# Index columns read in place, with a waited-for write of zeros between indirect transfers

## The chip, the cores and the metric

One core of a Trainium2 chip runs the whole program. The metric is the device time of one execution in microseconds (us). The kernel before takes 4911.03 us (median of three runs, 4899.02 to 4911.47). Everything below is read from one profiled execution of 4916.42 us.

## The reference

The input is a graph of 100,000 nodes with 64 features and 50,000 directed edges `src[e] -> dst[e]`, sorted by `dst`. Four blocks follow each other, each of the form "normalise, message passing, add":

```
h = relu(layernorm(x));  x = x + hop(hop(h))              # hop: segment_sum(edge_weight * h[src], dst)
h = relu(layernorm(x));  x = x + gcn(h @ W)               # degree-normalised sum, with self loops
h = relu(layernorm(x));  x = x + mlp(h + segment_sum(h[src], dst))
h = relu(layernorm(x));  x = x + update([h, segment_sum(message([h[src], h[dst], edge_attr]), dst)])
```

Rows of `x` have to be fetched by node number, and rows of the result have to be stored by node number. Both are done with indirect transfers, of which the program issues more than 2,700.

## The kernel before

The edges are laid out as 128 partitions by T = 392 columns; a unit is G = 14 columns, a step is two units (b = 0 and 1), and there are 14 steps per pass over the edges. An indirect transfer handles one column: 128 rows of 64 floats, one row for each partition, at the row numbers that stand in one column of an index tile. So a unit needs 14 gathers, and a pass 392.

GpSimd (POOL) issues every indirect transfer, in an order written out by hand. It passes through these stretches:

- From 25 us on, four units of rows of `x` are gathered (`gather_by_column`, call at L949), then `hop0` (L951 to L969) alternates accumulating scatters with gathers whose index slots VectorE has filled. `hop1` (L991 to L1005) holds accumulating scatters alone, up to about 2,116 us.
- 2,122 to 2,780 us: the first pass over the edges with gathered rows (loop at L1010, k = 0, table `xu`, index `map_idx`).
- 2,836 to 3,541 us: the same loop with k = 1, table `table0`, index `ptr_i`.
- 3,581 us to the end: the last pass. `t_gather` (L1046) gathers a step's rows from `table1` by `ptr_i`, `t_scatter` (L1053) stores a step's finished rows into `out` by `out_idx`. They take turns: gather of step i + 2 after scatter of step i - 1.

In the last three stretches, and at the very start, the 14 transfers of a unit are issued in the same way: `slot_copy` (L923 to L925) copies one index column (128 x 1 integers) from the wide tile (`dstc_i`, `map_idx`, `ptr_i` or `out_idx`) into a slot (`isl` or `osl`), raises `s_slot`, POOL waits for it, and issues the transfer with the slot as its index (L929 for gathers, L1062 for scatters). There are 1,624 such pairs of copy and transfer: 56 at the start, 392 in each of the two passes, and 784 in the last one.

What POOL waits for ahead of a unit: in the k = 0 pass, that VectorE has used the rows of the step before (`centred`); in the k = 1 and the last pass, `ga_free`, raised by VectorE when it has read the gathered rows. `t_scatter` waits for `o_ready` (the rows in `acc` are finished) and, from the second step on, also for `written[b]`: the scatters of the step before with the same slot have landed (L1058). ScalarE, which fills `acc`, waits for the same `written[b]` before it fills (L1666).

While POOL does this, VectorE, ScalarE and TensorE compute the rows of the nodes and edges step by step. VectorE's long operations are on 128 x 896 floats (a unit). Some take both inputs from SBUF (L2204, L2231, L2237), others one from SBUF and one from PSUM (L2214, L2222), others a single input (reductions, L2187).

Of the kernel before, what the change touches and what calls it, by code (L numbers as in the profile page):

```python
# [5 lines left out]
P = 128  # L6
# [8 lines left out]
G = 14  # L15
U = T // G
STEPS = U // 2
# [140 lines left out]
def gnn(nc, x, src, dst, edge_attr, edge_weight, W1g, b1g, W2a, b2a, W2b, b2b, mW1, mb1, mW2, mb2, uW1, ub1,  # L158
        uW2, ub2, out):
    ctx = ExitStack()  # L160
    with ctx:
        def sb(name, shape, dt=F32):
            return ctx.enter_context(nc.sbuf_tensor(name, shape, dt))

        def sem(name):
            return ctx.enter_context(nc.semaphore(name))

        def dram(name, shape):
            return nc.dram_tensor(name, shape, F32, kind="Internal").ap()


        tables = [dram(f"table{k}", [ROWS + P, D]) for k in range(2)]
# [48 lines left out]
        out_idx = sb("out_idx", [P, T], I32)  # L221
        dstc_i = sb("dstc_i", [P, T], I32)
        ptr_i = sb("ptr_i", [P, T], I32)
# [15 lines left out]
        hin, xw, h, vt, ga = (pair(n, unit) for n in ("hin", "xw", "h", "vt", "ga"))  # L239
# [4 lines left out]
        acc = pair("acc", unit)  # L244
# [25 lines left out]
        isl, osl = (pair(n, [P, G], I32) for n in ("isl", "osl"))  # L270
        isl_of = [*isl, *pair("isl_ahead", [P, G], I32)]
        hsum = sb("hsum", [P, D])
        fix = sb("fix", [P, 2 * D])
        brd = sb("brd", [P, 3 * D])
        bz = sb("bz", [P, 2 * P])
# [14 lines left out]
        ga_of = [*(t[:, :, :] for t in ga), ccu[0][2], ccu[1][2]]  # L290
# [87 lines left out]

        s_asked = sem("prep_operands_ready")
        s_answer = sem("prep_products_in_psum")  # L380
        s_slot = sem("pool_slot_copied")
        s_turned = sem("keys_turned")
        s_krow = sem("key_rows_ready")
        s_kept = [sem(f"edge_nodes_stored{b}") for b in range(2)]
# [68 lines left out]
        class Dense:  # L453
# [15 lines left out]
            copied = Ticks(sem("dense_copied"), [("h2", 0), ("y3", 1), ("h3", 1), ("h3", 0), ("y3", 0), ("h1", 1), ("h1", 0), ("h2", 1)],  # L469
                            [("h2", 0), ("y3", 1), ("h3", 1), ("h3", 0), ("y3", 0)])  # L470
# [13 lines left out]
        for k in range(2):  # L484
            sums = per_unit("m") if k == 0 else [("m", b, q) for b in B2K for q in range(HB)]
            f = Phase(f"hop{k}", [("l", B2K)] if k == 0 else [], per_unit("m"),
                      picked=per_half if k == 0 else None, compared=per_half,
                      merged=sums, sums=sums, slot=per_unit("i") if k == 1 else None,
                      in_free=per_unit("x") if k == 1 else None)
# [10 lines left out]
        for k in range(2):  # L500
            v = per_unit("v") if k == 1 else None
            v_back = v[::-1] if k == 1 else None
            f = Phase(f"s{k}", [("l", B2K)], v_back, turned=v_back, copied=v_back, product=v, taken=v,
                      ga_free=per_unit("g")[::-1] if k == 1 else None,
                      state_ready=per_unit("x"), acc_ready=per_unit("a"))
# [11 lines left out]
        tt = Phase("t", [("d1", B2K), ("d2", B2K), ("s3", B2K), ("d3", B2K)],  # L517
                   [*per_unit("vd", "us"), ("agg", 0), *per_unit("ud"), ("agg", 1), *per_unit("h3")],
                   turned=T_TURNED, copied=T_TURNED,
                   product=per_unit("m0", "m1", "vd", "us", "ud", "u0", "u1"),  # L520
                   hidden=T_MLP, second=T_MLP, message=per_unit("m0", "m1"),
                   taken=per_unit("vd", "us", "ud", "u0", "u1"), acc_ready=per_unit("a"),
                   in_free=per_unit("x"), gx_free=per_unit("g"), ga_free=per_unit("g"), o_ready=per_unit("o"),
                   early=T_EARLY, n=STEPS)
# [43 lines left out]
        def ecol(i, b):  # L568
            return (2 * i + b) * G

        def tcol(i, b):
            return (U - 1 - b) * G - 2 * G * i
# [287 lines left out]
        def _(pool):  # L860
            after = Settled(pool, s_passed)
# [58 lines left out]

                    after.wait_ge(s_sorted, 4 * 16 * SG * i + 4 * 16 * SG)

            def slot_copy(o, i_):  # L923

                return nc.gpsimd.tensor_copy(o, i_).then_inc(s_slot, 1)  # L925

            def gather(o, table, idx, s, columns=range(G)):
                for g in columns:
                    nc.gpsimd.indirect_dma_start(  # L929
                        o[:, g, :], None, table, bass.IndirectOffsetOnAxis(idx[:, g:g + 1], 0)).then_inc(s, 16)  # L930


            def gather_by_column(o, table, slot, index, c, s, copied):

                for g in range(G):
                    slot_copy(slot[:, g:g + 1], index[:, c + g:c + g + 1])
                    after.wait_ge(s_slot, copied + g + 1)
                    gather(o, table, slot, s, (g,))
                return copied + G

            after.wait_ge(s_node, 1)
            copied = 0

            hop_max, all_max = pool.to_reg(ROWS + 4 * P - 1), pool.to_reg(ROWS + N + 4 * P - 1)
            f = hops[0]
            for u in range(4):
                copied = gather_by_column(ga_of[u], x, isl_of[u], dstc_i, u * G, f.got[u], copied)  # L949

            def hop0(i):  # L951
                for b in B2K:
# [60 lines left out]
            for k, f in enumerate(sp_):  # L1013
                if k == 0:
                    table, index = xu, u_i
                else:
                    table, index = tables[k - 1], ptr_i
                    for b in B2K:
                        after.wait_ge(sp_[0].kept[b], 2 * 16 * STEPS)

                def body(i, first, copied):
                    for b in B2K if k == 0 else B2K[::-1]:
                        if not first:

                            if k == 0:
                                after.wait_ge(*f.centred.at(i - 1, ("l", b)))
                            else:
                                after.wait_ge(*f.ga_free.at(i - 1, ("g", b)))
                        copied = gather_by_column(ga[b], table, isl[b], index, ecol(i, b), f.got[b], copied)
                    return copied  # L1030

                for i in range(STEPS):
                    copied = body(i, i == 0, copied)

                for b in B2K:
                    after.wait_ge(f.stored[b], 16 * STEPS)
                nc.gpsimd.indirect_dma_start(hsum[:, :], None, tables[k], bass.IndirectOffsetOnAxis(head_i[:, :], 0),
                                             bounds_check=rows_max, oob_is_err=False).then_inc(s_head, 16)
                after.wait_ge(s_fix, k + 1)
                nc.gpsimd.indirect_dma_start(tables[k], bass.IndirectOffsetOnAxis(head_i[:, :], 0), fix[:, 0:D], None,  # L1040
                                             bounds_check=rows_max, oob_is_err=False).then_inc(s_fixed, 16)
                pool.dma_start(rows(tables[k])[:, EC * D:T * D], fix[:, D:2 * D]).then_inc(s_fixed, 16)
                after.wait_ge(s_fixed, 32 * (k + 1))


            def t_gather(i, copied, first=False):  # L1046
                for b in B2K:
                    if not first:
                        after.wait_ge(*tt.ga_free.at(i - 1, ("g", b)))
                    copied = gather_by_column(ga[b], tables[1], isl[b], ptr_i, tcol(i, b), tt.got_a[b], copied)  # L1050
                return copied

            def t_scatter(i, copied, first=False):  # L1053
                for b in B2K:
                    after.wait_ge(*tt.o_ready.at(i, ("o", b)))
                    if not first:

                        after.wait_ge(tt.written[b], 16 * G * i)  # L1058
                    for g in range(G):
                        slot_copy(osl[b][:, g:g + 1], out_idx[:, tcol(i, b) + g:tcol(i, b) + g + 1])  # L1060
                        after.wait_ge(s_slot, copied + b * G + g + 1)
                        nc.gpsimd.indirect_dma_start(  # L1062
                            out, bass.IndirectOffsetOnAxis(osl[b][:, g:g + 1], 0), acc[b][:, g, :], None,
                            bounds_check=nodes_max, oob_is_err=False).then_inc(tt.written[b], 16)
                return copied + 2 * G

            for q in LANES:
                after.wait_ge(s_dense[q], 16 * DSTEPS)
            copied = t_gather(0, copied, True)
            copied = t_gather(1, copied)  # L1070
            copied = t_gather(2, copied)
            copied = t_scatter(0, copied, True)
            copied = t_gather(3, copied)
            for i in range(2, STEPS - 2):
                copied = t_scatter(i - 1, copied)
                copied = t_gather(i + 2, copied)
            for i in (STEPS - 3, STEPS - 2):
                copied = t_scatter(i, copied)

            for b in B2K:  # L1080
                after.wait_ge(tt.kept[b], 16 * STEPS)
            nc.gpsimd.indirect_dma_start(hsum[:, :], None, suffix, bass.IndirectOffsetOnAxis(tail_i[:, :], 0),
                                         bounds_check=rows_max, oob_is_err=False).then_inc(s_head, 16)
            t_scatter(STEPS - 1, copied)
            after.wait_ge(s_border, 5)
            nc.gpsimd.indirect_dma_start(out, bass.IndirectOffsetOnAxis(brd_i[:, :], 0), fix[:, 0:D], None,
                                         bounds_check=nodes_max, oob_is_err=False).then_inc(s_final, 16)
# [1626 lines left out]
```

## Time and profile before

| | |
|---|---|
| median of three runs | 4911.03 us |
| profiled execution, its own time | 4916.42 us |
| its span, first to last instruction | 4914.2 us |
| POOL busy | 3807.9 us (77%) |
| PE (TensorE) busy | 3612.6 us (74%) |
| DVE (VectorE) busy | 3039.2 us (62%) |
| ACT (ScalarE) busy | 2012.8 us (41%) |
| granted TensorE clock, mean | 0.766 of full speed |

The profile names for each idle time of an engine what ended it, and follows the chain of work that ended last from the end of the program to its beginning. A duration of POOL in the profile is the time an instruction is recorded with; for an indirect transfer it is the time in which POOL makes the transfer's descriptors, not the time in which the data move. "issue" is time in which an engine waited for nothing that the profile shows.

### The profile page before, as it was taken

To read this page: it belongs to the slowest core of one execution; us is meant where nothing else is said; L and a number is where in the kernel's file an instruction comes from. 1 tells how busy PE (TensorE), PEld (TensorE's weight loads), DVE (VectorE), ACT (ScalarE), POOL (GpSimd) and SP (SyncE) were. 2 spreads that over 40 slices of the span, in tenths; PEclk is the share of its full clock that TensorE was granted. 3 is DMA by queue.
4 is the path that set the end of the run, shared out by engine and by line. 5 is a ranking of instruction groups with operands and counts; after the bars stand their busy time and mean duration, and the time that the engine had idled before them with its cause. 6 is when DMAs were issued, how large, how long until landed. Compare 5 with 4: busy or idle time off the path is not lost.

```text
span 4914.2 us, 62117 instructions
## 1 busy us (share of the span) xinstructions
PE 3612.6 (74%) x18706; PEld 2888.8 (59%) x18706; DVE 3039.2 (62%) x7232; ACT 2012.8 (41%) x5132; POOL 3807.9 (77%) x4405
## 2 busy tenths in 40 slices
PE   4767666666499999957777778878458787778784
PEld 2444344444399989945555556666346665656663
DVE  5634444444456566658888858888557666566661
ACT  3434434434311111135555555656225454454452
POOL 6788888888778888877788558888677888888875
PEclk8667767766655555578898989999779898998896
DMA  8433333332344454433343324444333223232220
GB/s 285 100 56 45 56 56 45 57 56 28 50 91 86 83 92 84 55 71 123 104 133 104 117 78 156 153 149 164 131 99 111 67 84 100 71 112 68 71 69 20
DMA packets 335499, 452.19 MB, mean 92 GB/s; under 512 B 208111, under 2 KB 233301, under 8 KB 334740
## 3 DMA queue, kind: packets, MB, share of 16 engines
q1 hardware_dynamic: 159268, 361.69, 20.9%
q0 software_dynamic: 176000, 87.72, 15.5%
q8 instruction: 109, 1.79, 0.2%
q14 instruction: 122, 1.00, 0.1%
HBM read 258.41 MB, written 225.53 MB: 98 GB/s over the span
## 4 chain that ended last, share of the span: by engine, by line
POOL 38%; issue 14%; PE 10%; DVE 6%; DMA 2%; ACT 2%; DVEq 0%; SPq 0%; POOLq 0%; ACTq 0%; another core or an unknown queue 0%
POOL ga L929 19%; POOL out_x L1062 8%; POOL isl L925 5%; POOL xu L1002 3%; PE tp L1259 2%; PE tp L1246 2%; POOL osl L925 2%; PE mm L1104 2%; PE mm L1123 1%; DMA xu<-acc,osl 1%; DVE xf L1948 1%; DVE wide L2107 1%; PE mm L1135 1%; PE mm L1097 1%; ACT zx L1597 1%
## 5 line engine op out<-in xcount | busy, mean ns | idle before, releaser
L929 POOL DMA_INDIRECT ga<-table,isl x784 | 838.8, 1070 | 224.4 <-issue 113.7
L1002 POOL DMA_INDIRECT xu<-acc,osl x392 | 625.1, 1595 | 144.8 <-issue 106.2
L1209 PE MATMUL tp<-xw,cc 128*128 128x394 f32 x784 | 411.5, 623 | 334.7 <-DVE cc L2015 243.3
L929 POOL DMA_INDIRECT ga<-xu,isl x392 | 424.1, 1082 | 111.8 <-POOL isl L925 61.5
L1062 POOL DMA_INDIRECT out_x<-acc,osl x392 | 418.6, 1068 | 114.5 <-POOL osl L925 80.8
L1209 PEld LDWEIGHTS tp<-xw,cc 128*128 128x128 f32 x784 | 141.3, 220 | 592.6 <-issue 324.9
L1246 PE MATMUL tp<-us,wide 128*128 128x64 f32 x1568 | 416.9, 422 | 88.9 <-DVE us L2143 50.0
L1246 PEld LDWEIGHTS tp<-us,wide 128*128 128x128 f32 x1568 | 379.9, 332 | 93.7 <-DVE us L2143 50.2
L1259 PE MATMUL tp<-acc,wide 128*128 128x64 f32 x1560 | 423.1, 427 | 0.8
L1194 PE MATMUL tp<-us,wide 128*128 128x64 f32 x1568 | 343.9, 421 | 69.6 <-DVE us L1932 60.8
L1562 ACT ACTIVATE acc<-tp,h 128x64 f32<-128x64 f32 x392 | 101.7, 310 | 693.2 <-PE tp L1259 541.9
L965 POOL DMA_INDIRECT hop_even<-acc,osl x196 | 322.1, 1643 | 81.2 <-issue 56.4
L1259 PEld LDWEIGHTS tp<-acc,wide 128*128 128x128 f32 x1560 | 371.8, 328 | 20.6 <-ACT acc L1562 5.8
L1194 PEld LDWEIGHTS tp<-us,wide 128*128 128x128 f32 x1568 | 337.8, 332 | 76.5 <-issue 76.5
L965 POOL DMA_INDIRECT hop_odd<-acc,osl x196 | 318.2, 1623 | 60.9 <-issue 57.9
L1097 PE MATMUL mm<-ident,wide 128*128 128x128 f32 x1176 | 196.8, 321 | 127.3 <-DVE wide L2204 59.0
L1104 PE MATMUL mm<-cc,u1s 128*128 128x512 f32 x448 | 213.7, 603 | 97.5 <-ACT zx L1597 76.1
L2055 DVE TENSOR_TENSOR osl<-sm,spare 128x14 int32<-128x14 f32 x28 | 4.9, 174 | 435.0 <-DMA hop_odd<-acc,osl 223.2
L1527 ACT ACTIVATE hin<-tp,xw 128x391 bf16<-128x391 f32 x392 | 233.0, 594 | 98.1 <-PE tp L1209 97.1
L1097 PEld LDWEIGHTS mm<-ident,wide 128*128 128x128 f32 x1176 | 167.0, 171 | 165.6 <-issue 88.8
L1540 ACT COPY acc<-tp 128x896 f32<-128x896 f32 x28 | 25.3, 905 | 580.7 <-DMA hop_odd<-acc,osl 256.6
L925 POOL COPY isl<-ptr_i 128x1 int32<-128x1 int32 x784 | 221.6, 283 | 50.8 <-DVE us L2231 40.0
(377 smaller groups left out, 9733.1 us busy)
## 6 DMA issues: line engine op xcount, KB each, us to landing
wide<-xu SPq DMA_DIRECT2D x84, 448.0 KB
zx<-key_rows SPq DMA_DIRECT2D x28, 896.0 KB
out_x<-wide SPq DMA_DIRECT2D x56, 448.0 KB
table<-acc SPq DMA_DIRECT2D x56, 448.0 KB
xf<-xs SPq DMA_DIRECT2D x56, 448.0 KB
wide<-table SPq DMA_DIRECT2D x56, 448.0 KB
xu<-in_x SPq DMA_DIRECT2D x25, 1000.0 KB
hop_even<-zeros SPq DMA_DIRECT2D x1, 12544.0 KB
```

Source lines behind the costliest of these rows:

```text
L925: return nc.gpsimd.tensor_copy(o, i_).then_inc(s_slot, 1)
L929: nc.gpsimd.indirect_dma_start(o[:, g, :], None, table, bass.IndirectOffsetOnAxis(idx[:, g:g + 1], 0)).then_inc(s, 16)
L965: nc.gpsimd.indirect_dma_start(hop[odd], bass.IndirectOffsetOnAxis(osl[b][:, g:g + 1], 0), acc[b][:, g, :], None, compute_op=ALU.add).then ...
L1002: nc.gpsimd.indirect_dma_start(xu, bass.IndirectOffsetOnAxis(osl[b][:, g:g + 1], 0), acc[b][:, g, :], None, compute_op=ALU.add).then_inc(f ...
L1062: nc.gpsimd.indirect_dma_start(out, bass.IndirectOffsetOnAxis(osl[b][:, g:g + 1], 0), acc[b][:, g, :], None, bounds_check=nodes_max, oob_i ...
L1097: t = nc.tensor.transpose(o[0:w, j * P:j * P + P], blk, ident[:, :])
L1104: t = nc.tensor.matmul(o[:, c:c + n], weights, flat(src_)[:, c:c + n], start=True, stop=extra is None)
L1194: t = nc.tensor.matmul(o[:, g * D:g * D + D], equal[b][:, c, (g % 2) * P:(g % 2) * P + P], us[b][:, c, :], start=n == 0, stop=n == 1)
L1209: f.key_row.raise_by(nc.tensor.matmul(tp[1][:, at:at + KEYS], reach[:, g * P:g * P + P], key_steps, start=True, stop=True), ("g", b, g))
L1246: t = nc.tensor.matmul(o, equal_run[:, 2 * q + n, mine:mine + P], us[b][:, 2 * q + n, :], start=n == 0, stop=alone and n == 1)
L1259: t = nc.tensor.matmul(o, equal_run[:, c, 2 * P + mine:3 * P + mine], passed[:, c, :], start=False, stop=n == 1)
L1527: nc.scalar.activation(sign_out[:, 2 * (g % 2), 0:EC], tp[1][:, at + 3:at + KEYS], ACT.Sign, bias=key_high[:, column], scale=-1.0, accum_o ...
```

## The change

The column copy goes. A transfer's index is now the column of the wide tile itself. In the copy's place, and in the same place of POOL's order, stands a write of zeros over a 128 x 128 float tile, `spacer`, which nothing reads. It raises the semaphore that the copy raised (renamed), and the transfer waits for it as before. In `t_scatter` the wait for `written[b]` goes as well, since no slot is overwritten. The slots `isl` and `osl` stay for `hop0` and `hop1`.

```
-            def slot_copy(o, i_):
-
-                return nc.gpsimd.tensor_copy(o, i_).then_inc(s_slot, 1)
...
-            def gather_by_column(o, table, slot, index, c, s, copied):
+            def gather_spaced(o, table, index, c, s, spaced):
 
                 for g in range(G):
-                    slot_copy(slot[:, g:g + 1], index[:, c + g:c + g + 1])
-                    after.wait_ge(s_slot, copied + g + 1)
-                    gather(o, table, slot, s, (g,))
-                return copied + G
+                    nc.gpsimd.memset(spacer[:, :], 0.0).then_inc(s_slot, 1)
+                    after.wait_ge(s_slot, spaced + g + 1)
+                    gather(o, table, index[:, c:c + G], s, (g,))
+                return spaced + G
...
-            def t_scatter(i, copied, first=False):
+            def t_scatter(i, spaced):
                 for b in B2K:
                     after.wait_ge(*tt.o_ready.at(i, ("o", b)))
-                    if not first:
-
-                        after.wait_ge(tt.written[b], 16 * G * i)
                     for g in range(G):
-                        slot_copy(osl[b][:, g:g + 1], out_idx[:, tcol(i, b) + g:tcol(i, b) + g + 1])
-                        after.wait_ge(s_slot, copied + b * G + g + 1)
+                        nc.gpsimd.memset(spacer[:, :], 0.0).then_inc(s_slot, 1)
+                        after.wait_ge(s_slot, spaced + b * G + g + 1)
                         nc.gpsimd.indirect_dma_start(
-                            out, bass.IndirectOffsetOnAxis(osl[b][:, g:g + 1], 0), acc[b][:, g, :], None,
+                            out, bass.IndirectOffsetOnAxis(out_idx[:, tcol(i, b) + g:tcol(i, b) + g + 1], 0),
+                            acc[b][:, g, :], None,
                             bounds_check=nodes_max, oob_is_err=False).then_inc(tt.written[b], 16)
```

POOL's row in the last pass, where the gathers of a unit end and the scatters of a step begin, before (`isl1` and `osl0` are the slots of unit 1 and unit 0):

```order
L929 DMA ga1<-table1,isl1 128x64 [waits pool_slot_copied]
L925 COPY isl1<-ptr_i 128x1
L929 DMA ga1<-table1,isl1 128x64 [waits pool_slot_copied]
L925 COPY osl0<-out_idx 128x1 [waits t_rows_written0,t_o_ready]
L1062 DMA out_x<-acc0,osl0 100000x64 [waits pool_slot_copied]
L925 COPY osl0<-out_idx 128x1
```

and the same place after the change:

```order
L926 DMA ga1<-table1,ptr_i 128x64 [waits pool_spacer_written]
L933 MEMSET spacer 128x128
L926 DMA ga1<-table1,ptr_i 128x64 [waits pool_spacer_written]
L1054 MEMSET spacer 128x128 [waits t_o_ready]
L1056 DMA out_x<-acc0,out_idx 100000x64 [waits pool_spacer_written]
L1054 MEMSET spacer 128x128
```

Each copy has become a write in its place; no transfer has moved, and the one wait for `t_rows_written` ahead of a step's scatters is gone. POOL has 3,718 rows in both orders, and the other engines keep theirs.

## Rows read from the trace of the kernel before

**Rows 1.** The page's chain that ended last, shares of the span by line.

```profile
POOL ga L929 19%; POOL out_x L1062 8%; POOL isl L925 5%; POOL xu L1002 3%; PE tp L1259 2%; PE tp L1246 2%; POOL osl L925 2%; PE mm L1104 2%; PE mm L1123 1%; DMA xu<-acc,osl 1%; DVE xf L1948 1%; DVE wide L2107 1%; PE mm L1135 1%; PE mm L1097 1%; ACT zx L1597 1%
```

**Rows 2.** Chain that ended last in 2122:2780, 2836:3541, 3740:4730, 4730:4914, shares of each.

```profile
by line: POOL ga L929 32.3%; issue 15.8%; POOL isl L925 7.9%; PE mm L1104 5.9%; PE mm L1123 3.7%; PE mm L1097 3.1%; ACT zx L1597 2.7%; PE mm L1135 2.6%; DMA ga<-xu,isl 2.3%; DVE st L2248 2.0%; ACT wide L1608 2.0%; DVE wide L2218 2.0%; DVE a
by line: POOL ga L929 56.1%; POOL isl L925 16.8%; issue 16.0%; PE mm L1123 2.1%; PE mm L1104 1.7%; PE mm L1097 1.3%; DMA hin<-ms 1.1%; PE mm L1135 0.9%; ACT wide L1608 0.5%; ACT zx L1597 0.4%; ACT cc L1589 0.4%; DMA ga<-table,isl 0.3%; DVE 
by line: POOL out_x L1062 33.3%; POOL ga L929 32.7%; issue 17.9%; POOL osl L925 8.3%; POOL isl L925 7.9%; POOLq L117 0.0%
by line: POOL out_x L1062 45.5%; issue 13.9%; POOL osl L925 10.0%; PE mm L1104 7.9%; PE mm L1123 4.9%; DMA out_x<-acc,osl 2.3%; ACT acc L1669 1.9%; DVE zx L1948 1.9%; PE tp L1097 1.7%; DVE st L2412 1.1%; ACT vt L1500 0.9%; POOLq L161 0.7%; 
```

**Rows 3.** Column copies (L925) by stretch: us, POOL busy (count), PEclk, DMA share, GB/s.

```profile
2122.00:2780.00 658.00, 105.08 (x392) 0.89 0.36 112
2836.00:3541.00 705.00, 122.75 (x392) 0.88 0.44 143
3740.00:4730.00 990.00, 156.07 (x614) 0.90 0.28 85
4730.00:4914.00 184.00, 17.83 (x83) 0.75 0.09 23
```

**Rows 4.** Copies by form in 2122:2780, 2836:3541, 3581:4914 (twice): busy us, mean ns.

```profile
L925 POOL COPY isl<-map_idx 128x1 int32<-128x1 int32 x392 | 105.4, 269 | 18.1 <-DVE xc L2255 13.6 <-DMA xu<-hsum 1.2
L925 POOL COPY isl<-ptr_i 128x1 int32<-128x1 int32 x392 | 122.8, 313 | 43.8 <-DVE us L2231 40.0 <-DMA table<-fix 1.3
L925 POOL COPY osl<-out_idx 128x1 int32<-128x1 int32 x392 | 99.2, 253 | 59.3 <-DVEq L80 57.5
L925 POOL COPY isl<-ptr_i 128x1 int32<-128x1 int32 x392 | 98.8, 252 | 7.0 <-DVEq L80 3.2 <-DMA table<-fix 1.3
```

**Rows 5.** All copies of L925: duration ns minimum/median/maximum, first and last start.

```profile
L925 POOL COPY isl<-ptr_i x784: 183/194/1111, 2835.9 to 4727.7; 128x1 int32<-128x1 int32 x196
L925 POOL COPY isl<-map_idx x392: 181/191/1116, 2121.7 to 2777.8; 128x1 int32<-128x1 int32 x196
L925 POOL COPY osl<-out_idx x392: 178/192/1164, 3734.0 to 4903.0; 128x1 int32<-128x1 int32 x196
```

**Rows 6.** Timeline of POOL and DVE near 3004 to 3014 us: start, us taken.

```profile
3003.63 1.09 DVE L2204 SCALAR_TENSOR_TENSOR wide<-wide,st 128x896 f32<-128x896 f32 x1
3003.74 1.02 POOL L925 COPY isl<-ptr_i 128x1 int32<-128x1 int32 x1
...
3005.03 0.97 POOL L929 DMA_INDIRECT ga<-table,isl  x1 [0.27 <-POOL isl L925]
...
3010.60 1.08 DVE L2231 TENSOR_TENSOR us<-hin,ga 128x896 f32<-128x896 f32 x1
...
3010.80 1.73 POOL L929 DMA_INDIRECT ga<-table,isl  x1 [0.27 <-issue]
...
3013.00 0.97 POOL L929 DMA_INDIRECT ga<-table,isl  x1 [0.27 <-POOL isl L925]
...
3013.43 1.09 DVE L2204 SCALAR_TENSOR_TENSOR wide<-wide,st 128x896 f32<-128x896 f32 x1
```

**Rows 7.** POOL's writes of constants at the start: start, us taken.

```profile
2.67 0.10 POOL L864 MEMSET kn_i<- 128x1 int32 x1
2.70 0.42 POOL L865 MEMSET wt<- 128x392 f32 x1
...
3.47 0.20 POOL L867 MEMSET ones<- 128x128 f32 x1
```

**Rows 8.** Two gathers with bounds whose index is a column of a tile.

```profile
L1082 POOL DMA_INDIRECT hsum<-suffix,tail_i x1 | 1.0, 1035 | 1.5 <-DMA suffix<-cc 1.5
L985 POOL DMA_INDIRECT fix<-hop_odd,ptr_i x1 | 1.0, 1022 | 0.3 <-issue 0.3
```

**Rows 9.** Waits in total, times, longest: for gathered rows, and for landed scatters.

```profile
DVE us L2231 <- DMA ga<-table,isl: 39.6, 12, 8.6
ACT acc L1669 <- DMA out_x<-acc,osl: 83.3, 8, 17.5
```

More of the change, by code:

```diff
@@ L272, in gnn @@
         hsum = sb("hsum", [P, D])
+        spacer = sb("spacer", [P, P])
         fix = sb("fix", [P, 2 * D])
@@ L380, in gnn @@
         s_answer = sem("prep_products_in_psum")
-        s_slot = sem("pool_slot_copied")
+        s_slot = sem("pool_spacer_written")
         s_turned = sem("keys_turned")
@@ L930, in gather @@
                         o[:, g, :], None, table, bass.IndirectOffsetOnAxis(idx[:, g:g + 1], 0)).then_inc(s, 16)
-            def gather_by_column(o, table, slot, index, c, s, copied):
+            def gather_spaced(o, table, index, c, s, spaced):
                 for g in range(G):
-                    slot_copy(slot[:, g:g + 1], index[:, c + g:c + g + 1])
-                    after.wait_ge(s_slot, copied + g + 1)
-                    gather(o, table, slot, s, (g,))
-                return copied + G
+                    nc.gpsimd.memset(spacer[:, :], 0.0).then_inc(s_slot, 1)
+                    after.wait_ge(s_slot, spaced + g + 1)
+                    gather(o, table, index[:, c:c + G], s, (g,))
+                return spaced + G
             after.wait_ge(s_node, 1)
-            copied = 0
+            spaced = 0
             hop_max, all_max = pool.to_reg(ROWS + 4 * P - 1), pool.to_reg(ROWS + N + 4 * P - 1)
@@ L948, in _ @@
             for u in range(4):
-                copied = gather_by_column(ga_of[u], x, isl_of[u], dstc_i, u * G, f.got[u], copied)
+                spaced = gather_spaced(ga_of[u], x, dstc_i, u * G, f.got[u], spaced)
             def hop0(i):
@@ L1019, in _, with body @@
                         after.wait_ge(sp_[0].kept[b], 2 * 16 * STEPS)
-                def body(i, first, copied):
+                def body(i, first, spaced):
                     for b in B2K if k == 0 else B2K[::-1]:
@@ L1028, in body @@
                                 after.wait_ge(*f.ga_free.at(i - 1, ("g", b)))
-                        copied = gather_by_column(ga[b], table, isl[b], index, ecol(i, b), f.got[b], copied)
-                    return copied
+                        spaced = gather_spaced(ga[b], table, index, ecol(i, b), f.got[b], spaced)
+                    return spaced
                 for i in range(STEPS):
-                    copied = body(i, i == 0, copied)
+                    spaced = body(i, i == 0, spaced)
                 for b in B2K:
@@ L1043, in _, with t_gather @@
                 after.wait_ge(s_fixed, 32 * (k + 1))
-            def t_gather(i, copied, first=False):
+            def t_gather(i, spaced, first=False):
                 for b in B2K:
@@ L1049, in t_gather @@
                         after.wait_ge(*tt.ga_free.at(i - 1, ("g", b)))
-                    copied = gather_by_column(ga[b], tables[1], isl[b], ptr_i, tcol(i, b), tt.got_a[b], copied)
-                return copied
-            def t_scatter(i, copied, first=False):
+                    spaced = gather_spaced(ga[b], tables[1], ptr_i, tcol(i, b), tt.got_a[b], spaced)
+                return spaced
+            def t_scatter(i, spaced):
                 for b in B2K:
                     after.wait_ge(*tt.o_ready.at(i, ("o", b)))
-                    if not first:
-                        after.wait_ge(tt.written[b], 16 * G * i)
@@ L1064, in t_scatter @@
                             bounds_check=nodes_max, oob_is_err=False).then_inc(tt.written[b], 16)
-                return copied + 2 * G
+                return spaced + 2 * G
             for q in LANES:
                 after.wait_ge(s_dense[q], 16 * DSTEPS)
[L1069 to L1073, printed above, removed]
+            spaced = t_gather(0, spaced, True)
@@ L1074, in _ @@
+            spaced = t_gather(1, spaced)
+            spaced = t_gather(2, spaced)
+            spaced = t_scatter(0, spaced)
+            spaced = t_gather(3, spaced)
             for i in range(2, STEPS - 2):
-                copied = t_scatter(i - 1, copied)
-                copied = t_gather(i + 2, copied)
+                spaced = t_scatter(i - 1, spaced)
+                spaced = t_gather(i + 2, spaced)
             for i in (STEPS - 3, STEPS - 2):
-                copied = t_scatter(i, copied)
+                spaced = t_scatter(i, spaced)
@@ L1083, in _ @@
                                          bounds_check=rows_max, oob_is_err=False).then_inc(s_head, 16)
-            t_scatter(STEPS - 1, copied)
+            t_scatter(STEPS - 1, spaced)
             after.wait_ge(s_border, 5)
```

## The prediction

> **What bounds the kernel now.** I read the chain of work that ended last first. It is the only view that says whose time is the program's time: POOL's gathers, scatters and column copies are the largest named entries on it, the copies alone at 5% and 2% of the span [rows 1]. The change touches only POOL in three passes, so the same chain is read by stretch next. In the k = 0 pass (2122 to 2780 us) it runs through POOL for about half the time, and through PE, ACT and DVE for the rest; in the k = 1 pass and between 3740 and 4730 us it is practically POOL alone [rows 2]. To see how many of the copies lie on it, take the chain's share of each stretch against all copies there [rows 2, 3]:
>
> - k = 0: 7.9% of 658 us is 52 us, of 105.08 us busy: 49% of 392 copies, about 194.
> - k = 1: 16.8% of 705 us is 118 us, of 122.75 us: 96%, about 378.
> - 3740 to 4730: 8.3% and 7.9% of 990 us are 160 us, against 156.07 us: all 614.
> - 4730 to the end: 10.0% of 184 us is 18 us, against 17.83 us: all 83.
>
> That makes 1,269 pairs on the path. The 56 pairs at the start and those from 3581 to 3740 us I count as off it.
>
> The third view is the copies' durations. The median is 191 to 194 ns and the longest over 1.1 us [rows 5], yet the means are 269, 313, 253 and 252 ns [rows 4]. A copy of one column has no reason to take a microsecond, so something holds it. The timeline of POOL beside DVE shows what: a copy that starts 0.11 us after a 1.09 us operation of DVE with two inputs in SBUF (L2204) takes 1.02 us and ends with it. The gather that starts at 3010.80, inside L2231 (both inputs in SBUF, until 11.68), takes 1.73 us instead of 0.97. But the gather of 3013.00 is in the middle of its work when L2204 begins at 3013.43, and still takes 0.97 us [rows 6]. So what waits is POOL's read, of the column or, at the start of a transfer, of the index; what POOL writes afterwards (the descriptors) passes.
>
> **The change, part by part.**
>
> *Removed: the copy's read.* The excess of the copies over their median is 392 x (269 - 191) ns = 30.6 us, 392 x (313 - 194) ns = 46.6 us, and for the last pass 392 x (253 - 192) and 392 x (252 - 194) ns, together 46.6 us [rows 4, 5]. On the path are 49%, 96% and 697/784 of that: 15 + 45 + 41 = 101 us. The new instruction reads nothing, so I take it that it is not held. Not all of the 101 us is won, because DVE's operation may still be running when the transfer reads its index. From the copy's place to that read go 0.20 us of the write, 0.27 us to the transfer's start, and about 0.12 us (the gather of 3010.80 was lengthened by 0.76 us, while DVE's operation had 0.88 us to run) [rows 6, 7]: 0.59 us. An operation of 1.09 us, met at a random point, has on average 0.545 us left, and beyond 0.59 us it has on average 0.50 x 0.50 / (2 x 1.09) = 0.115 us: 21% moves on to the transfer. I take a quarter, since transfers that used to start just after a held copy now meet DVE's operations at random. Gain: 0.75 x 101 = 76 us.
>
> *Added: the write of zeros.* A 128 x 128 write took 0.20 us (0.204 in the list of groups), against the copy's 0.192: 12 ns more, 1,269 x 0.012 = 15 us. The trace shows none behind a transfer. From the other side: a one-column write is recorded with 0.10 us, but the next one starts 0.03 us after it [rows 7], so up to 0.07 us of a recorded duration can lie beside a neighbour. If it did here, a pair would be 0.06 us shorter than now, -76 us in all. I take +15 us, because the transfer waits for the write's end, not its start; both ends stay in the range.
>
> The Trainium skill bears on the first of these parts from both sides. "SBUF — State Buffer", section "Who interferes with whom", says that a VectorE instruction with two SBUF inputs contends with a GpSimd instruction that reads SBUF, not with one that only writes it. The same page's "Terms" describes the port pair the two share as an exclusive lock, held for the whole instruction, under which the loser fully blocks. By the first the sum stays as it stands; by the second the gain of 76 us is absent and rival A's time holds. The rows on descriptors speak for the first; no row has a plain write beside such an operation.
>
> *Changed: where the index lies.* The transfer now reads its column in a row of 392, not of 14. One transfer before does so, L985 with `ptr_i`, at 1022 ns, 50 ns over the usual 0.97; but it has bounds, and L1082, whose index tile is one column wide, has 1035 [rows 8]. So the width is probably not what costs. Between 0 and 0.05 us a transfer, 0 to +63 us; I take 0.
>
> *Removed: the wait for landed scatters.* ACT waits for the same count before it fills `acc`, and it is ACT that is seen waiting, 83.3 us in 8 waits [rows 9]. POOL's wait is over whenever ACT has begun. It costs nothing now and gives nothing.
>
> *Queued behind.* The write stands where the copy stood, and the transfer waits for it alone; nothing else on POOL is passed, and SP's queue has no part.
>
> *What is late next.* In the k = 1 pass DVE is waiting for gathered rows, 39.6 us in 12 waits, 3.3 us each [rows 9]. A step of 28 pairs gains 28 x (0.119 x 0.75 - 0.012) = 2.2 us, less than that. So the consumer can follow. In the k = 0 pass half the chain is elsewhere, which the 49% has taken off.
>
> **The sum.** -76 + 15 = -61 us. The profiled execution took 4916.42 us, so it would take 4855. The median of the runs shown is 5.4 us below it; from 4911.03 the forecast is **4850 us**, 1.2% faster.
>
> **The rivals.**
>
> *A. The write is held as well.* For it speaks that no plain write of POOL is seen beside a two-input operation; against it the gather of 3013.00 [rows 6]. The copies' holds then stay, the 12 ns come on top (15 us), and a write of 128 columns is exposed about 0.10 us longer than one of one column [rows 7]. In the k = 1 pass a copy loses 0.119 us on average, or 0.119 / 0.545 = 22% are caught, which is 0.2 such operations per us; 0.10 us more exposure catches 2% more, each for about 1.09 us: 0.022 x 1,269 = 28 us. Sum +43: 4954 us, slower. Decided by whether a write inside L2204 is longer than 0.20 us.
>
> *B. The index in place costs.* At 0.05 us a transfer 63 us come back: -61 + 63 = +2, 4913 us, no change.
>
> *C. The loop is held by others.* POOL gets faster, but in part of the passes DVE, ACT and PE are the next bound at once, as in half of the k = 0 pass already [rows 2]. If half the gain goes this way: 4881 us. Against it are the waits of DVE and ACT for POOL's transfers [rows 9].
>
> *D. The write overlaps the transfer's end*, the -76 us of above in place of +15: 101 x 0.75 + 76 = -152 us, 4759 us. For it only the overlap among writes speaks [rows 7]; a copy, which waits for the same transfer, shows none.
>
> **Chances.** The forecast 0.46, A 0.14, B 0.10, C 0.17, D 0.13. The forecast's own range is 4825 to 4880 us (a gain of 36 to 86 us: holds moving on by nothing or by half, and the 49% of the first pass off by half). The range for 8 in 10 reaches halfway to D and part of the way to A: 4790 to 4930 us. Less than 0.3% (15 us) can't be told from no change. Faster by more: the forecast, C and D, 0.75; within: B and the weak end of A and C, 0.12; slower: most of A and a costlier B, 0.13.
>
> **What would show it.** If right: the writes have a mean close to their median of about 0.20 us, also inside L2204; the transfers' mean rises from 1.08 us by about 0.02 us, and their undisturbed length stays at 0.97; the stretch from 3740 to 4730 shortens by about 20 us (36 us of holds, a quarter kept, 7 us for the longer writes) and the k = 1 pass by about 30. Writes near 1 us would be A, transfers with a shortest time near 1.02 us B, shorter POOL work with new waits for DVE ahead of units C, and less than 0.46 us from one transfer's end to the next one's start D. The forecast fails if two-input operations of DVE are lengthened by the writes instead.

## The result, and the profile after

The changed kernel takes 4823.79 us (median of four runs, 4821.91 to 4828.70) against 4907.63 us for the kernel before (four runs): a ratio of 0.9833, 95% interval 0.9816 to 0.9850, 84 us faster. The forecast was 4850 us. The median lies 1 us outside the forecast's own range (4825 to 4880 us) and inside the range for 8 in 10 (4790 to 4930 us). The profiled execution took 4822.62 us, 94 us less than that of before.

The copies' rows [rows 4] and the transfers, by stretch. First what the rows of before did not yet show, the transfers of the kernel before in the k = 0 pass, the k = 1 pass and the last pass (busy us, mean ns, then idle time ahead of them):

```profile
L929 POOL DMA_INDIRECT ga<-xu,isl x392 | 424.1, 1082 | 111.8 <-POOL isl L925 61.5 <-issue 50.4
L929 POOL DMA_INDIRECT ga<-table,isl x392 | 426.2, 1087 | 112.6 <-POOL isl L925 58.5 <-issue 54.1
L1062 POOL DMA_INDIRECT out_x<-acc,osl x392 | 418.6, 1068 | 114.5 <-POOL osl L925 80.8 <-issue 33.7
L929 POOL DMA_INDIRECT ga<-table,isl x392 | 412.6, 1053 | 111.8 <-issue 59.6 <-POOL isl L925 52.2
```

The same stretches of the changed kernel, transfers and writes (k = 0, k = 1, then four groups of the last pass):

```profile
L926 POOL DMA_INDIRECT ga<-xu,map_idx x392 | 405.7, 1035 | 112.2 <-POOL spacer L933 106.6 <-issue 5.7
L933 POOL MEMSET spacer<- 128x128 f32 x392 | 85.5, 218 | 26.5 <-DVE xc L2250 24.9 <-DMA xu<-hsum 1.2
...
L926 POOL DMA_INDIRECT ga<-table,ptr_i x392 | 439.1, 1120 | 113.9 <-POOL spacer L933 107.1 <-issue 6.8
L933 POOL MEMSET spacer<- 128x128 f32 x392 | 85.6, 218 | 39.0 <-DVE us L2226 37.4 <-DMA table<-fix 1.3
...
L1056 POOL DMA_INDIRECT out_x<-acc,out_idx x392 | 433.7, 1106 | 114.6 <-POOL spacer L1054 108.6 <-issue 6.0
L926 POOL DMA_INDIRECT ga<-table,ptr_i x392 | 396.9, 1012 | 111.9 <-POOL spacer L933 106.0 <-issue 6.0
L1054 POOL MEMSET spacer<- 128x128 f32 x392 | 92.4, 236 | 53.0 <-DVEq L80 53.0
L933 POOL MEMSET spacer<- 128x128 f32 x392 | 85.9, 219 | 4.8 <-DVEq L80 3.2 <-DMA table<-fix 1.3
```

Add busy and idle time of a stretch. k = 0: 659 us before [rows 4], 630 after, 29 less. k = 1: 705 and 678, 28 less. Last pass: 1322 and 1293, 29 less. That is 86 of the 94 us between the two profiled executions; where the other 8 us lie is left open. The forecast's terms by stretch were 9, 29 and 23 us.

All writes of L933, and the gathers of L926 with the index in place: minimum/median/maximum in ns.

```profile
L933 POOL MEMSET spacer<- x1232: 198/218/326, 25.0 to 4633.2; 128x128 f32 x176
...
L926 POOL DMA_INDIRECT ga<-table,ptr_i x784: 949/950/1864, 2806.6 to 4633.7; - x196
L926 POOL DMA_INDIRECT ga<-xu,map_idx x392: 949/950/1797, 2119.5 to 2746.7; - x196
```

No write took longer than 0.33 us, where copies reached 1.16 us [rows 5]. VectorE's two-input operations did not grow longer in exchange, which was the forecast's sign of failure: the median of `wide<-wide,st` is 1091 ns before (L2204) and after (L2199). Transfers are still held, up to 1.86 us. The timeline of POOL and DVE around the operation that held the copy in [rows 6] (now L2199) shows both:

```profile
2972.06 1.08 DVE L2226 TENSOR_TENSOR us<-hin,ga 128x896 f32<-128x896 f32 x1
2972.39 1.58 POOL L926 DMA_INDIRECT ga<-table,ptr_i  x1 [0.27 <-POOL spacer L933]
...
2974.89 1.09 DVE L2199 SCALAR_TENSOR_TENSOR wide<-wide,st 128x896 f32<-128x896 f32 x1
...
2975.41 0.22 POOL L933 MEMSET spacer<- 128x128 f32 x1
...
2975.90 0.95 POOL L926 DMA_INDIRECT ga<-table,ptr_i  x1 [0.27 <-POOL spacer L933]
```

The write of 2975.41 lies wholly inside a two-input operation and takes its usual 0.22 us; the gather of 2972.39, whose index read falls into one, takes 1.58 us. This is the rule of the Trainium skill's "SBUF — State Buffer", section "Who interferes with whom" (only GpSimd instructions that read SBUF contend with two inputs of VectorE); its "Terms", by which the loser of the shared port pair fully blocks, does not hold for this write.

### The profile page after: what moved, and what is told of

Its sections match the earlier page's. It is cut to its first block, busy times and chain, and to the rows that moved or that the text cites. A ratio compares the mean times of both kernels' runs of the same rounds, so it can differ in the third digit from the quotient of the medians.

```text
span 4820.3 us, 62091 instructions
## 1 busy us (share of the span) xinstructions
PE 3571.8 (74%) x18706; PEld 2862.3 (59%) x18706; DVE 3027.6 (63%) x7232; ACT 2009.3 (42%) x5132; POOL 3709.4 (77%) x4405
## 4 chain that ended last, share of the span: by engine, by line
POOL 38%; issue 12%; PE 9%; DVE 8%; DMA 3%; ACT 2%; DVEq 0%; SPq 0%; POOLq 0%; ACTq 0%
POOL ga L926 20%; POOL out_x L1056 9%; POOL spacer L933 4%; POOL xu L999 3%; PE tp L1254 2%; POOL spacer L1054 2%; PE tp L1241 2%; PE mm L1099 2%; DMA xu<-acc,osl 2%; DVE xf L1943 1%; PE mm L1118 1%; DVE wide L2102 1%; PE mm L1130 1%; DVE acc L1943 1%; ACT zx L1592 0%
## 5 line engine op out<-in xcount | busy, mean ns | idle before, releaser
L926 POOL DMA_INDIRECT ga<-table,ptr_i x784 | 836.0, 1066 | 225.8 <-POOL spacer L933 213.1
L1056 POOL DMA_INDIRECT out_x<-acc,out_idx x392 | 433.7, 1106 | 114.6 <-POOL spacer L1054 108.6
L926 POOL DMA_INDIRECT ga<-xu,map_idx x392 | 405.7, 1035 | 112.2 <-POOL spacer L933 106.6
L933 POOL MEMSET spacer<- 128x128 f32 x1232 | 269.4, 219 | 84.9 <-DVE us L2226 37.4
L1092 PEld LDWEIGHTS mm<-ident,wide 128*128 128x128 f32 x1176 | 156.6, 164 | 155.0 <-DVE wide L2199 88.0
```

Source lines behind the costliest of these rows:

```text
L926: nc.gpsimd.indirect_dma_start(o[:, g, :], None, table, bass.IndirectOffsetOnAxis(idx[:, g:g + 1], 0)).then_inc(s, 16)
L933: nc.gpsimd.memset(spacer[:, :], 0.0).then_inc(s_slot, 1)
L1092: t = nc.tensor.transpose(o[0:w, j * P:j * P + P], blk, ident[:, :])
```

## The experiments

Each ratio is to the kernel before, timed beside it on the same chip. The chips differ from one group of experiments to the next, so kernels are compared by their ratios, not by their us. "Pause" is the time from one transfer's end to the next one's start when nothing is held: 0.19 + 0.27 = 0.46 us before, 0.22 + 0.27 = 0.49 us after the change.

**A read in the write's place.** Two kernels ask whether the read was the cost. The first copies a column that nobody uses, with the index in place:

```
-  nc.gpsimd.memset(spacer[:, :], 0.0).then_inc(s_slot, 1)
+  nc.gpsimd.tensor_copy(spare_slot[:, g:g + 1], index[:, c + g:c + g + 1]).then_inc(s_slot, 1)
```

> The write of zeros is replaced by a copy of one column (128 x 1) into a slot that nobody uses; the index is still read in place. Theory 1, the gain is the read that DVE's two-input operations held: the copies are held again (mean 0.25 to 0.31 us, longest over 1 us), and the time is within 25 us of the kernel before, 4880 to 4907 us. Theory 2, the gain is the index read in place: the time stays near the changed kernel, 4824 us, and the copies' mean does not matter.

Measured: ratio 0.9999 (0.9989 to 1.0009), 4915.44 against 4918.04 us, as theory 1 had it. The whole gain is gone, so the index in place is worth nothing by itself. This kernel has the shorter pause of before, so read and pause are not yet apart. The second keeps the pause of the changed kernel and reads:

```
-  nc.gpsimd.memset(spacer[:, :], 0.0).then_inc(s_slot, 1)
+  nc.gpsimd.tensor_copy(spacer[:, 0:40], spacer[:, 64:104]).then_inc(s_slot, 1)
```

> The spacer is a copy inside the spacer tile, 40 columns to 40 columns, that takes about as long undisturbed as the write of zeros (0.22 us); index in place. It reads, so DVE's two-input operations hold it. Theory 1 (the gain is the removed hold): the time is that of the kernel before plus 0.03 us on each of 1,269 pairs, 4900 to 4950 us. Theory 4 (the gain is the pause of 0.49 us between two transfers in place of 0.46; pauses of 0.38 to 0.40 us cost 8 to 9%, of 0.30 us 17%): the time stays at 4824 to 4845 us.

Measured: ratio 1.0048 (1.0031 to 1.0065), 4937.34 us, as theory 1 had it. Its reading spacers by duration, and by mean:

```profile
L933 POOL COPY spacer<-spacer x1232: 213/221/1162, 25.3 to 4742.5; 128x40 f32<-128x40 f32 x176
...
L933 POOL COPY spacer<-spacer 128x40 f32<-128x40 f32 x1232 | 384.7, 312 | 53.7 <-DVE us L2228 36.7 <-DVEq L80 3.3 <-DMA table<-fix 2.5
L1056 POOL COPY spacer<-spacer 128x40 f32<-128x40 f32 x392 | 112.4, 287 | 49.3 <-DVEq L80 49.1
```

The median, 221 ns, is about that of the write (218), the mean is 91 ns above it. Between this kernel and the changed one only read or write differs, and the ratios differ by 0.0215, 105 us. Some 26 us of that are the gathers, whose undisturbed length is 971 and 976 ns behind the copies of this kernel and 950 ns behind the write. Between this kernel and the one before lie the longer pause and a copy that is held a little more (83 ns above its median on average, against 79 ns): 0.0048, 24 us slower. So, taken in this order, the change is -105 and +24 us.

The order matters, as a kernel further below shows, with a write of 96 columns and so the pause of before:

| ratio to the kernel before | pause 0.46 us | pause 0.49 us |
|---|---|---|
| spacer reads | 0.9999 | 1.0048 |
| spacer writes | 0.9894 | 0.9833 |

Taking the read away first gives -52 us (0.9999 to 0.9894), and the longer pause then -30 us (0.9894 to 0.9833). So the removed read gains 52 to 105 us; the longer pause costs 24 us with reading spacers and gains 30 us with writing ones. The two are not independent, and neither split is the true one.

**The index from slots, with writes between.** One copy of 14 columns per unit fills a slot, the write stands before each transfer, the wait for landed scatters is back:

```
+  nc.gpsimd.tensor_copy(slot[:, :], index[:, c:c + G]).then_inc(s_slot, 1)
   for g in range(G):
       nc.gpsimd.memset(spacer[:, :], 0.0).then_inc(s_slot, 1)
-      gather(o, table, index[:, c:c + G], s, (g,))
+      gather(o, table, slot, s, (g,))
```

> The index comes from a slot again, but a slot of 14 columns is filled by one copy per unit (112 copies in place of 1,568), and the write of zeros stands before each transfer; the wait for landed scatters is back because slots are overwritten. Theory 1: 4824 us plus at most 112 x 0.3 = 34 us for the copies and 1,269 x 0.02 = 25 us if the transfers' undisturbed length (0.950 us in the changed kernel, 0.971 before) belongs to the index in place: 4835 to 4880 us. Theory 2: the gain is lost, 4895 us or more.

Measured: ratio 0.9869 (0.9847 to 0.9890). The gain stays, less 18 us, which the 112 copies may cost (the two intervals touch). That is theory 1. Its gathers, and those of the first kernel above (copy between, index in place):

```profile
L926 POOL DMA_INDIRECT ga<-table,isl x784: 949/952/1877, 2809.1 to 4655.8; - x196
```

```profile
L927 POOL DMA_INDIRECT ga<-table,ptr_i x784: 966/973/1893, 2838.9 to 4722.1; - x196
```

An undisturbed gather takes 0.95 us behind a write and 0.97 us behind a copy, wherever its index lies. Scatters show no such difference: 979 ns by the median before the change, 981 ns after it.

**The wait put back.** The changed kernel with `after.wait_ge(tt.written[b], 16 * G * i)` ahead of a unit's scatters.

> The changed kernel with POOL's wait for landed scatters put back ahead of each unit's scatters. Theory 1: no difference, 4824 us within 10 us, since ScalarE has waited for the same count before. Theory 3, that a part of the gain came from this wait: 4835 us or more and new idle time of POOL ahead of the scatters.

Measured: ratio 0.9839 (0.9819 to 0.9859), the same as the changed kernel's within the noise. The removed wait was worth nothing that can be told.

**No write, no pause.** Both lines between two transfers are left out:

```
-  nc.gpsimd.memset(spacer[:, :], 0.0).then_inc(s_slot, 1)
-  after.wait_ge(s_slot, spaced + g + 1)
```

> No write and no wait between two transfers; index in place. Theory 1: a pair of 0.22 + 0.27 + 0.95 us becomes 0.30 + 0.97 us as in the stretch where transfers follow each other directly, 0.17 us less; over the 1,269 pairs on the path -215 us if nothing else binds, and DVE (80% busy in the k = 1 pass) and PE leave about half of it: 4650 to 4750 us. Rival: transfers that follow each other directly are slower in these passes (held longer, or the queue fills), and the spacing is worth its time: 4820 us or more, with a mean transfer over 1.25 us.

Measured: ratio 1.1706 (1.1668 to 1.1744), 5755.04 us. I had expected the largest gain of all; my theory fell here. The rival's time came true, but not its reason, since the transfers themselves were not slower (0.98 and 1.04 us on average). POOL now waits for DVE, at hundreds of us that were not there:

```profile
POOL out_x L1052 <- DVEq L80: 650.9, 14, 50.7
...
DVE mean_row L2450 <- remote: 526.7, 16, 49.7
POOL ga L926 <- DVE us L2222: 437.3, 13, 66.6
...
POOL ga L926 <- DVE xc L2246: 276.1, 13, 29.2
```

"remote" is a releaser that the profile could not find. The timeline of all engines in the k = 1 pass shows why DVE was late:

```profile
3193.01 3.35 PE L1095 MATMUL mm<-cc,u1s 128*128 128x512 f32 x4 [6.04 <-issue]
...
3199.53 0.49 PE L1128 MATMUL tp<-wg,vt 128*128 128x65 f32 x2
...
3200.53 0.94 POOL L926 DMA_INDIRECT ga<-table,ptr_i  x1 [0.30 <-issue]
...
3208.01 0.94 POOL L926 DMA_INDIRECT ga<-table,ptr_i  x1 [0.30 <-issue]
3209.62 1.09 DVE L2235 TENSOR_TENSOR xw<-xf,tp 128x896 f32<-128x896 f32 x1 [13.70 <-remote]
...
3212.46 1.01 ACT L1588 ACTIVATE zx<-mm,bcol 128x896 f32<-128x896 f32 x1 [16.97 <-remote]
```

ACT's operation of 3212.46 waits on TensorE's semaphore alone, for the matmuls of L1095, which were over at 3196.36 (3193.01 + 3.35): it starts 16.1 us later. DVE's operation of 3209.62 reads a product (`tp`) whose last matmul is over by 3200.02 (3199.53 + 0.49), and starts 9.6 us later, 0.67 us after the last of POOL's transfers in a row (3208.01 + 0.94). By the program it waits for two stores as well, but those were issued before 3145, and in the changed kernel such stores land within 3 to 4 us by the median. The same is seen 50 us earlier: the matmuls that ACT's L1588 waits for are over at 3145.87, POOL's row of transfers at 3149.54, and ACT starts at 3152.04. So TensorE's signals are acted on late by DVE and ACT while POOL's transfers follow each other at 0.30 us; DVE is then late to free the rows, and POOL waits for it. Whether the signal leaves TensorE late or arrives late the traces don't show. The granted TensorE clock is lower in this run, 0.726 against 0.764 beside it; but PE is busy for only 131 us more (3743.4 against 3612.6 us), so slower matmuls don't explain some 840 us. Four kernels ask what it is in the pause that lets the signals through.

**A wait that is long reached**, no write: `after.wait_ge(s_node, 1)` ahead of each transfer.

> No write; each transfer carries a wait for a semaphore that was reached at the start of the program. If a wait of any kind is enough, as at the borders between units in the run without writes, the pair is 0.95 + 0.30 us and the time 4600 to 4750 us. If the wait must be for something not yet reached, the time is that of the run without writes, 5700 to 5800 us.

Measured: ratio 1.1703 (1.1660 to 1.1746), that of no write. A wait on paper makes no pause; the transfers still follow at 0.30 us.

**The write, not waited for.** The transfer waits for the write before the last one.

> The 128-column write stays before each transfer, but the transfer waits for the write before the last one, which is long done. If the write alone keeps TensorE's signals on time, the 0.27 us between write and transfer shrink and the time falls to 4650 to 4800 us. If it is the pause in which POOL waits that lets them through, they are late again and the time rises towards that without a write, 5100 us or more.

Measured: ratio 1.0923 (1.0882 to 1.0964), 5352.88 us: the write alone is not enough. The timeline shows the pause, 0.22 + 0.17 us:

```profile
2299.11 0.95 POOL L926 DMA_INDIRECT ga<-xu,map_idx  x1 [0.17 <-issue]
2300.06 0.22 POOL L935 MEMSET spacer<- 128x128 f32 x1
2300.44 0.95 POOL L926 DMA_INDIRECT ga<-xu,map_idx  x1 [0.17 <-issue]
```

**A write of one column**, waited for: `memset(spacer[:, 0:1], 0.0)`.

> The changed kernel with a write of one column in place of 128. Without any write TensorE's signals to DVE and ACT came up to 20 us late while POOL's transfers followed each other, and on time with it. Theory 1 (the write only has to separate two transfers; its length is a plain cost): a pair is about 0.10 us shorter, 1,269 x 0.10 = 127 us at most, and 4700 to 4770 us. Rival: the signals need the time that the write takes, and a shorter one brings late signals back: above 4824 us.

Measured: ratio 1.0829 (1.0780 to 1.0878). The write takes 0.11 us, so the pause is 0.38 us. The theory of the plain cost was wrong again, and the rival's time came.

**The full write before every second transfer** (`if g % 2 == 0:` ahead of both lines): pauses of 0.30 and 0.49 us in turn.

> The 128-column write and its wait before every second transfer only. A pair of transfers takes 0.22 + 0.27 + 0.95 + 0.30 + 0.95 us, 0.10 us less per transfer, 1,269 x 0.10 = 120 us at most if TensorE's signals are held only until the next write, at most some 2.5 us: 4720 to 4820 us. If a late signal costs more than that, above 4824 us.

Measured: ratio 1.0545 (1.0481 to 1.0609), 5182.24 us. That is the second case: late signals cost more than the shorter pauses save.

**96, 112 and 160 columns.** The first and the last bracket the change, the one in the middle was chosen from their results.

> The changed kernel with a write of 96 columns (0.19 us), so the pause is 0.46 us as in the kernel before, and nothing is read. Theory 1: 0.027 us less on 1,269 pairs, 34 us: 4785 to 4810 us. Theory 4: the pause of the kernel before brings its time back: 4880 to 4920 us or more.

> The changed kernel with a write of 160 columns (0.25 us), a pause of 0.52 us. Theory 1: 34 us more, 4850 to 4865 us. Theory 4, if 0.49 us is not yet enough: 4780 to 4830 us, less than the plain cost of the longer write.

> The changed kernel with a write of 112 columns, a pause between those of 96 and 128 columns (0.475 us). Plain cost alone: 17 us less than the changed kernel, ratio to before 0.980. If shorter pauses cost more than they save from 0.49 us down, as the run with 96 columns (ratio 0.9894) says, the ratio lies between 0.983 and 0.989.

Measured: 96 columns 0.9894 (0.9871 to 0.9916), 4856.23 us, single runs from 4833.81 to 4873.64 us; 112 columns 0.9804 (0.9791 to 0.9817), 4804.27 us; 160 columns 0.9876 (0.9859 to 0.9892), 4854.82 us. With 96 columns neither theory came true: the time lies between the two forecasts. With 160 columns theory 1 did, and with 112 columns the plain cost alone (0.980), not the range of 0.983 to 0.989. From 112 through 128 to 160 the time rises by 0.0029 and 0.0043, 14 and 21 us, where the writes alone are 21 and 45 us longer (13 and 28 ns on each of 1,624). From 112 to 96 it rises by 0.0090, 44 us, where they are 21 us shorter. POOL's waits for DVE ahead of units say where, first with 96 columns (its profiled execution is the fastest of the four, so it shows less than the median would), then with 112:

```profile
POOL spacer L933 <- DVE us L2226: 69.1, 10, 47.7
POOL spacer L933 <- DVE xc L2250: 46.9, 12, 10.0
```

```profile
POOL spacer L933 <- DVE us L2226: 39.9, 1, 39.9
POOL spacer L933 <- DVE xc L2250: 23.1, 9, 5.0
```

Put together, for spacers that write: pauses of 0.30, 0.38 and 0.39 us give 1.17, 1.08 and 1.09; 0.46 us gives 0.989; 0.48, 0.49 and 0.52 us give 0.980, 0.983 and 0.988. The best of these is the write of 112 columns, faster than the kernel before by 2.0% and, by the two ratios, than the changed kernel by 0.3%, though their intervals touch (0.9791 to 0.9817 and 0.9816 to 0.9850). That the pause decides in the main is shown by this row of runs; why TensorE's signals need it is not.

The waits that the profile puts down to "remote" follow the same row. Over the whole program those of DVE and ACT add up to some 1,680 us without a write, 960 us with one column, 180 us with 96, 2 us with 160, and none with 112 and 128. (The index from slots has 12 us and the wait put back 55 us, both at the pause of 0.49 us, so the row is not a strict one.) The kernel before has 123 us of them, of which this is the largest group, then that of the kernel with 96 columns, then the same line in the changed kernel:

```profile
DVE acc L2428 <- remote: 24.7, 9, 3.1
```

```profile
DVE acc L2423 <- remote: 65.9, 18, 11.3
```

```profile
DVE acc L2423 <- PE mm L1118: 213.1, 28, 22.7
```

If these waits are late signals here too, as they are where the timeline above was read, the kernel before already had some, and the change took them away. With reading spacers they come to 104 us at a pause of 0.46 us and 8 us at 0.49 us, yet the second kernel is 0.5% slower. So they cost nothing that can be told there, and why a pause of 0.46 us costs time with writes and not with reads stays open.

## Why the prediction was right

*What bounds the kernel, and what goes with the read.* The step held: the held reads were a cost, and it went with them. The term of the sum was -76 us, 101 us of excess less a quarter. The kernels that differ in read or write alone give -105 us at the pause of 0.49 us and -52 us at 0.46 us, and some 26 us of either are the shorter gathers. So the term lies inside what was measured, and the runs give its size no more closely than that. Rival A is refuted by the longest write (0.33 us) and by the write inside L2199.

*A quarter moves on to the transfer.* About right over the whole, though not pass by pass. Take a transfer's mean less its undisturbed length, before and after. In the k = 1 pass that rose by 54 ns (1087 - 971 to 1120 - 950), with the scatters by 36 ns (1068 - 979 to 1106 - 981); in the k = 0 pass it fell by 22 ns and with the last pass's gathers by 20 ns. Together that is 19 us more, 15% of the copies' 124 us. The sign that was named for it did not come: the transfers' mean stayed at 1.07 us, since the undisturbed gathers became 21 to 25 ns shorter. On 1,176 gathers that is some 26 us, and it stood in no term of the sum. Rival B had it the other way round.

*The write's cost.* 12 ns a pair, 15 us, was too little. The write takes 218 ns among transfers and 236 ns before scatters, not 204; the comparison with the reading spacer of the same length puts the longer pause at 24 us, of which some 7 us can be longer holds (83 less 79 ns on each of 1,624). Rival D, the overlap, did not come: the pause is 0.22 + 0.27 us in full.

*The share on the path.* This is the step that failed most in size. "k = 0: 49%" gave 9 us for a pass that gave 29; these 20 us are most of the 23 by which the forecast's gain of 61 us fell short of 84. All copies of the pass on the path would have made it 18 us (0.75 x 30.6 - 4.7); the transfers, 18 us shorter in all (424.1 to 405.7 us) where they were forecast longer, did more than fill the rest, and new waits for DVE took 11 us back. The waits of the k = 0 pass, before and then after (us in total, times, longest), show what the share of 49% hid:

```profile
DVE st L2248 <- DMA ga<-xu,isl: 27.2, 10, 8.2
```

```profile
DVE st L2243 <- DMA ga<-xu,map_idx: 14.5, 7, 6.8
```

DVE waited for gathers in this pass as POOL waited for DVE: the first fell by 13 us, the second rose only from 13.6 us [rows 4] to 24.9 us, while POOL's own work shrank by 38 us. By this reading the consumers of the gathers came earlier too, and so the pass gave 29 of the 38 us that POOL won. Rival C, built on the same reading as the 49%, shows only in these 11 us of new waits for DVE.

*The wait for landed scatters, the index in place, what is late next.* As forecast: nothing, nothing, and the consumers followed.

*Luck in the sum.* The terms missed in both directions: the write was priced too low, the shorter gathers not at all, and the k = 0 pass at a third. Their errors cancelled in part, and the total came nearer than the terms.

*What the forecast did not see.* It priced the spacer as a cost alone. It is the condition for the rest of the program to run: without it, or with a pause below 0.4 us, the kernel is 8 to 17% slower. With 96 columns the same way of pricing said 34 us faster than the change, and the chip was 30 us slower (the ratios are 0.0061 apart). The number did not hang on that alone: with the pause of before, and the write, the time would be 0.9894 of 4911.03, or 4859 us, which is in the range too. But that the write was long enough at all was luck as far as the prediction goes, for nothing in it spoke against a shorter one.

## What to carry to other kernels

Compare an instruction's mean with its median before you price it: an operation of one column that is sometimes a microsecond long is being held, and on GpSimd it may be enough to let it write where it read. Before taking out an instruction that seems only to cost time between two indirect transfers, try it: here, with less of a gap, TensorE's signals were acted on late. Where two engines take turns in waiting for each other, as in the k = 0 pass, a saving can be worth more than the share of its engine in the chain that ended last.

## What the hardware showed that was not expected

- While POOL issued indirect transfers 0.30 us apart, signals of TensorE were acted on 9.6 us (DVE) and 16.1 us (ACT) after the matmuls' ends, once the row of transfers was over. A signal of ACT to DVE passed in the same stretch: DVE's `st` of L2178 began at 3193.84, 0.03 us after ACT's `cc` of L1564 (3192.86 + 0.95).
- With writing spacers the effect is steep: from 0.48 to 0.46 us of pause costs 0.9%, to 0.38 us another 9%.
- An undisturbed gather takes 0.950 us behind a write and 0.971 to 0.978 us behind a copy; a scatter 0.98 us behind either.
- Between gathers, a write of 96, 112, 128 and 160 columns takes 0.193, 0.206, 0.219 and 0.247 us on average; none took over 0.36 us, so none was held by DVE's two-input operations of 1.09 us.
